# Gathers tied to TensorE's progress: two added waits before each pair of indirect DMA asks in a recommender head

## The chip, the cores and the metric

One core of one Trainium2 chip. The metric is device time in microseconds (us) from launch to end; one execution is also taken by the hardware profiler, which gives the span from the first to the last instruction. Engines: TensorE (PE; its weight loads are PEld), VectorE (DVE), ScalarE (ACT), GpSimd (POOL), SyncE (SP), and 16 DMA engines.

## What is computed

2,048 (user, item) pairs. Both indices pick an embedding row of 32 numbers; two small layers with ReLU follow, and a head over 1,250 items with a sigmoid:

```python
all_embed = jnp.concatenate([users_emb_w[users], items_emb_w[items]], axis=1)   # 2048 x 64
h = jax.nn.relu(all_embed @ w1.T + b1)                                          # 2048 x 128
h = jax.nn.relu(h @ w2.T + b2)                                                  # 2048 x 128
cross = jax.nn.one_hot(items, NUM_ITEMS, dtype=h.dtype)
head_in = jnp.concatenate([cross, h], axis=1)
return jax.nn.sigmoid(head_in @ w_head.T + b_head)                              # 2048 x 1250
```

All in float32. The one-hot part of the head is a lookup: it adds row `items` of the transposed head weights to the logits. The host lays each item's embedding and its head row side by side in `item_rows` (1,282 numbers), so one gather brings both.

## The kernel before

The 2,048 pairs are 16 tiles of 128 (`TILES`, `LAST` = 15), one pair to a partition. For tile t the work is a line through all engines:

- POOL (lines 155 to 172 of the profile's numbering) asks for two indirect DMAs: the item rows (L165, 128 rows of 5,128 bytes) and the user rows (L169, 128 rows of 128 bytes), both into tile t's own place in `rows`. Both raise the semaphore `s_rows[t]` by 16 when they have landed. Before the item ask of tile t stands one wait, on the landing of both gathers of tile t-4 (`IN_FLIGHT` = 4). POOL does nothing else after its first microseconds. `rows` has room for all 16 tiles, so no ask waits for a buffer.
- DVE `split_emb(t)`: waits for `s_rows[t]` at 32 and for `s_xT`, casts the embedding into a high part (L204, tile `emb`) and subtracts for the low part (L206). PE `transpose(t)` (L298, into `ps_x`) raises `s_xT`; DVE `copy_embT(t)` (L210) takes it to `embT`.
- PE `layer_1(t)` (L306 and L307, into `ps_h`): the second matmul raises `s_l1`. ACT `relu_1` (L259), PE `layer_2` (L311), ACT `relu_2` (L263, L268), DVE `split_h2` (L214).
- PE, the head: four passes (L315) of three matmuls each into `acc`: bias, high x high, high x low, low x high. DVE `add_rows` (L223) adds the gathered head row, ACT `sigmoid` (L273) follows, and SP writes the tile out (L150), in halves for tiles 0 to 14. Tile 15 is done in three column chunks; ACT asks for the last write (L292).

All orders are written out by hand. In PE's loop, for t from 1 to 14: bias pass of t, layer 1 of t+1, high pass of t, layer 2 of t+1, high-low pass of t, transpose of t+2, low pass of t. DVE's loop: `add_rows(t-1)`, `split_emb(t+2)`, `copy_embT(t+2)`, `split_h2(t+1)`. Semaphores `s_xT` and `s_l1` rise by one a tile, in the order of tiles.

Of the kernel before, what the change touches and what calls it, by code (L numbers as in the profile page):

```python
# [8 lines left out]
IN_FLIGHT = 4  # L9
# [10 lines left out]
def rec_head_kernel(nc, pairs, user_rows, item_rows, w1T, b1, w2T, b2, w_hiddenT, b_head, out):  # L20
# [30 lines left out]
    with ExitStack() as ctx:  # L51
# [6 lines left out]
        def sem(name):  # L58
            return ctx.enter_context(nc.semaphore(name))
# [52 lines left out]
        s_xT = sem("s_xT")  # L112
        s_embT = sem("s_embT")
        s_l1 = sem("s_l1")
# [19 lines left out]
        @block.sync  # L134
        def _(sp):
            sp.dma_start(idx[:], pairs_v).then_inc(s_idx, 16)
            sp.dma_start(bias_f[:], bias_v).then_inc(s_bhead, 16)
            for half in range(2):
                sp.dma_start(w1T_f[half * K1:(half + 1) * K1, :], w1T).then_inc(s_w1, 16)
            sp.dma_start(w2T_sb[:], w2T).then_inc(s_w2, 16)  # L140
            sp.wait_ge(s_const, 3)
            sp.wait_ge(s_bias_split, 2)
            for r, part in enumerate((bias_hi, bias_lo)):
                sp.dma_start(bias_parts[r:r + 1, :].bitcast(F32).rearrange("a (p c) -> a p c", p=BP),
                             part[:].bitcast(F32)).then_inc(s_bias_row, 16)

            for t in range(TILES):
                for i, (c, n) in enumerate(parts[t][:-1] if t == LAST else parts[t]):
                    sp.wait_ge(s_prob, parts_until(t - 1) + i + 1)
                    sp.dma_start(out_v[:, t * N + c:t * N + c + n], logits(t, c, n)).then_inc(s_out, 16)  # L150
            sp.wait_ge(s_out, 16 * parts_until(LAST))

        @block.gpsimd
        def _(pool):
            nc.gpsimd.memset(ident[:], 0.0).then_inc(s_zero, 1)
            pool.wait_ge(s_zero, 1)
            nc.gpsimd.affine_select(out=ident[:], in_=ident[:], compare_op=ALU.not_equal, fill=1.0, base=0,
                                    pattern=[[-1, P]], channel_multiplier=1).then_inc(s_ident, 1)
            pool.wait_ge(s_idx, 16)
            for t in range(TILES):  # L160

                if t >= IN_FLIGHT:
                    pool.wait_ge(s_rows[t - IN_FLIGHT], 32)
                at = t * ROW
                nc.gpsimd.indirect_dma_start(  # L165
                    out=rows[:, at + UD:at + ROW], out_offset=None, in_=item_rows,
                    in_offset=bass.IndirectOffsetOnAxis(ap=idx[:, 2 * t + 1:2 * t + 2], axis=0),
                ).then_inc(s_rows[t], 16)
                nc.gpsimd.indirect_dma_start(  # L169
                    out=rows[:, at:at + UD], out_offset=None, in_=user_rows,  # L170
                    in_offset=bass.IndirectOffsetOnAxis(ap=idx[:, 2 * t:2 * t + 1], axis=0),
                ).then_inc(s_rows[t], 16)
# [241 lines left out]
```

## Time and profile before

| | |
|---|---|
| three runs | 66.87, 66.89, 67.44 us (median 66.89) |
| the profiled execution | 66.53 us, span 64.7 us |
| PE busy | 56.9 us, 88% of the span |
| DVE busy | 42.3 us, 65% |
| ACT busy | 39.4 us, 61% |
| POOL busy | 31.2 us, 48% |
| DMA | 21.86 MB, mean 338 GB/s |
| item asks, user asks | 16 and 16, 0.95 us each on POOL |

An engine's busy time says how much it did, not whether the end waited for it. The chain of waits follows the last instruction back to what released it, step by step; the time lies there. The list of waits names who waited for whom. In a timeline each line is an instruction (or several of one kind) with its start, its duration and, in brackets, the idle time of the engine before it and what ended that. "issue" there is idle time in which the engine waited for nothing that the profile shows.

### The profile page before, as it was taken

The numbers are of one execution on the slowest core, as the hardware profiler recorded it, in microseconds if no ns is written. First come the engines' busy times: TensorE is split into PE (matmuls) and PEld (weight loads), VectorE is DVE, ScalarE is ACT, GpSimd is POOL, SyncE is SP. The second block draws the span as 40 slices with busy tenths as digits, with TensorE's granted clock in tenths as the row PEclk, the third lists the DMA queues.
The fourth block names the chain that finished last, engine by engine and source line by source line (L and its number), as shares of the span: only waits on it lengthen the run. The fifth ranks groups of instructions, "written<-read, shape, count | busy, mean of one in ns | idle before, by whom it ended". The sixth has DMA issues, their size and how long they took to land.

```text
span 64.7 us, 906 instructions
## 1 busy us (share of the span) xinstructions
PE 56.9 (88%) x284; PEld 43.3 (67%) x284; DVE 42.3 (65%) x107; ACT 39.4 (61%) x85; POOL 31.2 (48%) x38
## 2 busy tenths in 40 slices
PE   0999997899999999999999999999999999996000
PEld 1444425786688888888788877888888888774000
DVE  3810227547796969696886979696968769489000
ACT  0622921426949595776959594958678595959400
POOL 4288688778868877886887787650000000000000
PEclk9999999999999999999999999999999999999955
DMA  0589989988889999999999999999999999999980
GB/s 0 54 303 305 322 330 240 245 352 181 279 238 371 411 399 417 383 371 403 407 412 414 421 400 411 413 412 418 417 410 382 393 380 386 385 382 348 379 310 28
DMA packets 8512, 21.86 MB, mean 338 GB/s; under 512 B 1596, under 2 KB 2236, under 8 KB 8508
## 3 DMA queue, kind: packets, MB, share of 16 engines
q0 software_dynamic: 2816, 10.77, 46.5%
q1 hardware_dynamic: 5116, 10.29, 42.2%
q10 hardware_dynamic: 576, 0.76, 4.0%
q8 instruction: 2, 0.03, 0.2%
q14 instruction: 2, 0.02, 0.1%
HBM read 11.56 MB, written 10.24 MB: 337 GB/s over the span
## 4 chain that ended last, share of the span: by engine, by line
PE 67%; DMA 10%; ACT 6%; DVE 5%; issue 2%; POOL 2%; ACTq 0%
PE acc L315 52%; PE ps_h L311 8%; DMA rows<-user_rows,idx 7%; ACT rows L273 4%; DVE rows L223 4%; PE ps_x L298 4%; DMA idx<-pairs 3%; PE ps_h L307 3%; PE ps_h L306 2%; POOL rows L165 2%; DVE emb L206 1%; ACT h1T L259 1%; ACT h2T_hi L263 1%; DVE emb L204 0%; ACT h2T_f L268 0%
## 5 line engine op out<-in xcount | busy, mean ns | idle before, releaser
L223 DVE TENSOR_TENSOR rows<-acc,rows 128x625 f32<-128x625 f32 (+2 forms) x33 | 24.4, 783 | 1.2 <-PE acc L315 0.2
L273 ACT ACTIVATE rows<-rows 128x625 f32<-128x625 f32 (+2 forms) x33 | 23.1, 705 | 0.9 <-DVE rows L223 0.8
L165 POOL DMA_INDIRECT rows<-item_rows,idx x16 | 15.3, 956 | 6.0 <-issue 4.6
L169 POOL DMA_INDIRECT rows<-user_rows,idx x16 | 15.3, 954 | 4.9 <-issue 4.9
L259 ACT ACTIVATE h1T<-ps_h,b_sb 128x128 f32<-128x128 f32 x16 | 5.9, 368 | 14.5 <-PE ps_h L307 14.5
L315 PE MATMUL acc<-w_hid_lo,h2T_hi 128*128 128x512 f32 (+1 forms) x45 | 12.2, 380 | 0.0
L315 PE MATMUL acc<-w_hid_hi,h2T_lo 128*128 128x512 f32 (+1 forms) x45 | 12.1, 377 | 0.0
L315 PE MATMUL acc<-w_hid_hi,h2T_hi 128*128 128x512 f32 (+1 forms) x45 | 11.7, 369 | 0.0
L315 PE MATMUL acc<-bias_parts,bias_sel 128*128 128x512 f32 (+1 forms) x45 | 11.3, 358 | 0.0
L210 DVE CAST embT<-ps_x 128x128 fp32r<-128x128 f32 x16 | 4.7, 292 | 8.5 <-PE ps_x L298 8.5
L353 PE MATMUL ps_x<-warm_pe 128*128 128x512 f32 x12 | 8.1, 849 | 1.5 <-DVE warm_pe L176 1.5
L311 PE MATMUL ps_h<-h1T,w2T_sb 128*128 128x128 f32 x32 | 7.8, 325 | 0.6 <-ACT h1T L259 0.6
L315 PEld LDWEIGHTS acc<-bias_parts,bias_sel 128*128 128x128 f32 x45 | 7.3, 189 | 1.2
L315 PEld LDWEIGHTS acc<-w_hid_hi,h2T_lo 128*128 128x128 f32 x45 | 7.5, 193 | 0.7
L315 PEld LDWEIGHTS acc<-w_hid_lo,h2T_hi 128*128 128x128 f32 x45 | 7.4, 191 | 0.7
L315 PEld LDWEIGHTS acc<-w_hid_hi,h2T_hi 128*128 128x128 f32 x45 | 7.4, 191 | 0.6
L353 PEld LDWEIGHTS ps_x<-warm_pe 128*128 128x128 f32 x12 | 3.2, 280 | 5.5 <-issue 4.1
L311 PEld LDWEIGHTS ps_h<-h1T,w2T_sb 128*128 128x128 f32 x32 | 4.8, 188 | 2.9 <-issue 0.7
L263 ACT ACTIVATE h2T_hi<-ps_h,b_sb 128x128 fp32r<-128x128 f32 x16 | 5.9, 366 | 1.2 <-PE ps_h L311 1.2
L268 ACT ACTIVATE h2T_f<-ps_h,b_sb 128x128 f32<-128x128 f32 x16 | 5.8, 360 | 0.0
L214 DVE TENSOR_TENSOR h2T_lo<-h2T_f,h2T_hi 128x128 fp32r<-128x128 f32 x16 | 4.6, 286 | 1.1 <-ACT h2T_f L268 1.1
L298 PE MATMUL ps_x<-ident,emb 128*128 128x128 f32 x16 | 4.5, 284 | 0.3 <-DVE emb L206 0.2
(35 smaller groups left out, 39.3 us busy)
## 6 DMA issues: line engine op xcount, KB each, us to landing
probs<-rows SPq DMA_DIRECT2D x30, 312.5 KB, 7.5
w_hid_f<-w_hiddenT ACTq DMA_DIRECT2D x1, 625.0 KB, 4.4
probs<-rows SPq DMA_DIRECT2D x2, 256.0 KB, 3.2
rows<-item_rows,idx POOLq DMA_INDIRECT x16, 7.0
rows<-user_rows,idx POOLq DMA_INDIRECT x16, 7.2
probs<-rows ACTq DMA_DIRECT2D x1, 113.0 KB, 3.7
w1T_f<-w1T SPq DMA_DIRECT2D x2, 32.0 KB
w2T_sb<-w2T SPq DMA_DIRECT2D x1, 64.0 KB, 4.6
```

The source lines that it names most:

```text
L165: nc.gpsimd.indirect_dma_start(out=rows[:, at + UD:at + ROW], out_offset=None, in_=item_rows, in_offset=bass.IndirectOffsetOnAxis(ap=idx[: ...
L169: nc.gpsimd.indirect_dma_start(out=rows[:, at:at + UD], out_offset=None, in_=user_rows, in_offset=bass.IndirectOffsetOnAxis(ap=idx[:, 2 * ...
L210: nc.vector.tensor_copy(embT[:], ps_x[:, 0:P]).then_inc(s_embT, 1)
L223: nc.vector.tensor_tensor(logits(t, c, n), acc[t % SLOTS][:, c:c + n], logits(t, c, n), ALU.add).then_inc(s_sum, 1)
L259: nc.scalar.activation(h1T[:], ps_h[:, 0:P], ACT.Relu, bias=b1_sb[:]).then_inc(s_h1, 1)
L263: nc.scalar.activation(h2T_hi[t % SLOTS][:], ps_h[:, P:2 * P], ACT.Relu, bias=b2_sb[:]).then_inc(s_h2_hi, 1)
L268: nc.scalar.activation(h2T_f[:], ps_h[:, P:2 * P], ACT.Relu, bias=b2_sb[:]).then_inc(s_h2, 1)
L273: nc.scalar.activation(logits(t, c, n), logits(t, c, n), ACT.Sigmoid).then_inc(s_prob, 1)
L298: nc.tensor.transpose(ps_x[:, 0:P], emb[:], ident[:]).then_inc(s_xT, 1)
L311: nc.tensor.matmul(ps_h[:, P:2 * P], w2T_sb[:], h1T[:], start=True, stop=True).then_inc(s_l2, 1)
L315: last = nc.tensor.matmul(acc[t % SLOTS][:, c:c + n], h, w[:, c:c + n], start=first, stop=end)
L353: nc.tensor.matmul(ps_x[:], warm_pe[:, 0:P], warm_pe[:], start=True, stop=True)
```

## The change

POOL gets two more waits for each of tiles 5 to 15. Before the item ask of tile t it waits until the transpose of tile t-4 is done, beside the wait that it has on the landing of t-4; between the item ask and the user ask it waits until the first layer of tile t-4 is done. The asks themselves, their order and their destinations are the same, and no other engine's code changes.

```diff
@@ -161,11 +161,17 @@
 
                 if t >= IN_FLIGHT:
                     pool.wait_ge(s_rows[t - IN_FLIGHT], 32)
+
+
+                if t > IN_FLIGHT:
+                    pool.wait_ge(s_xT, t - IN_FLIGHT + 1)
                 at = t * ROW
                 nc.gpsimd.indirect_dma_start(
                     out=rows[:, at + UD:at + ROW], out_offset=None, in_=item_rows,
                     in_offset=bass.IndirectOffsetOnAxis(ap=idx[:, 2 * t + 1:2 * t + 2], axis=0),
                 ).then_inc(s_rows[t], 16)
+                if t > IN_FLIGHT:
+                    pool.wait_ge(s_l1, t - IN_FLIGHT + 1)
                 nc.gpsimd.indirect_dma_start(
                     out=rows[:, at:at + UD], out_offset=None, in_=user_rows,
                     in_offset=bass.IndirectOffsetOnAxis(ap=idx[:, 2 * t:2 * t + 1], axis=0),
```

## Rows read from the trace of the kernel before

**Rows 1.** The page's part 4, the chain that ended last, by engine.

```profile
PE 67%; DMA 10%; ACT 6%; DVE 5%; issue 2%; POOL 2%; ACTq 0%
```

**Rows 2.** Busy time by stretch; the last three columns are granted clock, DMA share, GB/s.

```profile
20.00:49.50 29.50, 29.50 (x171) 24.65 (x169) 23.61 (x59) 21.61 (x51) 17.42 (x19) 1.00 1.03 406
49.50:58.00 8.50, 8.50 (x47) 6.99 (x47) 6.21 (x16) 6.19 (x15) 0.00 (x0) 1.00 1.04 386
...
58.60:59.20 0.60, 0.60 (x6) 0.51 (x4) 0.60 (x2) 0.60 (x2) 0.00 (x0) 1.00 0.80 292
```

**Rows 3.** The list of waits: us in total, times, longest.

```profile
POOL rows L169 <- issue: 4.9, 16, 0.3
POOL rows L165 <- issue: 4.6, 15, 0.3
```

**Rows 4.** POOL timeline: user ask of tile 8, item ask of 10, asks of 13 to 15.

```profile
24.42 0.95 POOL L169 DMA_INDIRECT rows<-user_rows,idx  x1 [0.30 <-issue]
...
28.22 0.95 POOL L165 DMA_INDIRECT rows<-item_rows,idx  x1 [0.30 <-issue]
...
35.74 0.94 POOL L165 DMA_INDIRECT rows<-item_rows,idx  x1 [0.30 <-issue]
36.98 0.94 POOL L169 DMA_INDIRECT rows<-user_rows,idx  x1 [0.30 <-issue]
38.23 0.94 POOL L165 DMA_INDIRECT rows<-item_rows,idx  x1 [0.30 <-issue]
39.48 0.94 POOL L169 DMA_INDIRECT rows<-user_rows,idx  x1 [0.31 <-issue]
40.72 0.94 POOL L165 DMA_INDIRECT rows<-item_rows,idx  x1 [0.30 <-issue]
41.97 0.94 POOL L169 DMA_INDIRECT rows<-user_rows,idx  x1 [0.30 <-issue]
```

**Rows 5.** DVE's timeline: casts of `emb` for tiles 7, 8, 10, 11 and 15.

```profile
28.61 0.18 DVE L204 CAST emb<-rows 128x64 fp32r<-128x64 f32 x1
...
31.67 0.20 DVE L204 CAST emb<-rows 128x64 fp32r<-128x64 f32 x1
...
37.52 0.43 DVE L204 CAST emb<-rows 128x64 fp32r<-128x64 f32 x1
...
40.64 0.18 DVE L204 CAST emb<-rows 128x64 fp32r<-128x64 f32 x1
...
52.47 0.18 DVE L204 CAST emb<-rows 128x64 fp32r<-128x64 f32 x1
```

**Rows 6.** Line 169, the eight user asks from 24.3 to 42.1 us: ask to landing.

```profile
DMA to landing us min/median/max: 7.2/7.5/7.7
```

**Rows 7.** The chain in order of time, between the index's landing and POOL's first ask.

```profile
2.63 0.28 issue
```

**Rows 8.** PE's timeline: transposes of tiles 9, 10, 11, first layers of the same tiles.

```profile
35.19 0.27 PE L298 MATMUL ps_x<-ident,emb 128*128 128x128 f32 x1
...
36.52 0.27 PE L307 MATMUL ps_h<-embT,w1T_lo 128*128 128x128 f32 x1
...
38.26 0.33 PE L298 MATMUL ps_x<-ident,emb 128*128 128x128 f32 x1
...
39.64 0.28 PE L307 MATMUL ps_h<-embT,w1T_lo 128*128 128x128 f32 x1
...
41.28 0.28 PE L298 MATMUL ps_x<-ident,emb 128*128 128x128 f32 x1
...
42.61 0.27 PE L307 MATMUL ps_h<-embT,w1T_lo 128*128 128x128 f32 x1
```

**Rows 9.** Tile `emb`: all 16 casts, ns min/median/max.

```profile
L204 DVE CAST emb<-rows x16: 182/184/428, 9.1 to 52.5; 128x64 fp32r<-128x64 f32 x16
```

**Rows 10.** Landing: ACT's last write (page, part 6), and SP's 32 writes.

```profile
probs<-rows ACTq DMA_DIRECT2D x1, 113.0 KB, 3.7
...
DMA to landing us min/median/max: 2.9/7.2/12.3
```

## The prediction

> **What bounds the kernel now.** I read the page's chain of waits first, then the busy time by stretch. The chain is TensorE's own work for two thirds of the span [rows 1], and from 20 to 58 us TensorE is busy all the time [rows 2]: one matmul follows the other. What stands outside it is the start (index load, first item ask, its landing) and the end (last additions, sigmoids, last write). So the time can only move if the change makes TensorE wait, or moves the end behind the last matmul.
>
> Then the list of waits, for POOL. The idle time before its two asks is 0.3 us each time and is put down to "issue", not to a semaphore; the wait on the landing of tile t-4, which stands before each item ask, never shows as a releaser [rows 3]. POOL runs free: two asks cost 38.23 to 40.72 = 2.49 us a tile [rows 4]. The period of the other engines is read from DVE's casts of `emb`: 40.64 to 52.47 is four tiles, 2.96 us each [rows 5]. POOL gains some 0.47 us on TensorE with every tile and so is early at the end, not late.
>
> Then the DMA. From 20 to 49.5 us its share is 1.03 at 406 GB/s, and from 49.5 to 58 us, with writes alone, still 1.04 at 386 GB/s [rows 2]. It is a second limit just under the first: only at 58.6 to 59.2 us does the share dip to 0.80, when the backlog of writes is used up shortly before the last tile's come. In this load a gather of user rows lands 7.2 to 7.7 us after its ask [rows 6].
>
> **What the change adds.** Nothing is removed or moved. For tiles 5 to 15 two waits are added, 22 in all. Behind the waiting instruction on POOL stand only the later asks; SP, ACT and their queues issue nothing behind it. Who waits for the asks is DVE's cast of `emb`, then the transpose, so TensorE.
>
> *When do the waits bite?* First how fast POOL starts behind a wait: the first ask begins 0.28 us after the index landed [rows 7]. Behind a semaphore of TensorE no row shows it. I bound it by 0 below (it starts at once) and 0.30 us above, the gap before any ask [rows 4]. I take 0.28, POOL's own row.
> - Item ask 13 needs transpose 9, which ends at 35.19 + 0.27 = 35.46; plus 0.28 is 35.74. The ask of before starts at 35.74 [rows 4, 8]: delay 0. Each earlier tile has 0.47 us more of margin (tile 12 0.47, tile 5 over 3), so no earlier wait bites.
> - User ask 13 needs first layer 9: 36.52 + 0.27 + 0.28 = 37.07 against 36.98: 0.09 late.
> - Item ask 14: 38.26 + 0.33 + 0.28 = 38.87 against 38.23: 0.64 late. User ask 14: 39.64 + 0.28 + 0.28 = 40.20 against 39.48: 0.72 late.
> - Item ask 15: 41.28 + 0.28 + 0.28 = 41.84 against 40.72: 1.12 late. User ask 15: 42.61 + 0.27 + 0.28 = 43.16 against 41.97: 1.19 late. At the lower bound for the start, user ask 15 is only 42.88 - 41.97 = 0.91 us late.
>
> So the change acts on five asks of 32.
>
> *What covers the delay?* The last ask lands at 43.16 + 7.7 = 50.86 us, and the cast that reads it starts at 52.47 [rows 5, 6]: 1.6 us left. For tile 14, one tile earlier, 40.20 + 7.7 = 47.9 against 52.47 - 2.96 = 49.51: again 1.6. This would not get worse if the waits bit from tile 5 on: the ask would then follow first layer t-4 by 0.28 us, and the cast of tile t follows first layer t-1 by 40.64 - (39.64 + 0.28) = 0.72 us, three periods later: 3 x 2.96 + 0.72 - 0.28 = 9.3 us against 7.7. The landing would have to take 1.6 us longer for the cover to be gone; each us beyond is then paid once. Cost: 0.
>
> *What do the added waits cost when satisfied?* The item asks of before carry one wait, the user asks none, and the gap before both is 0.30 us (35.74 and 36.98 are such a pair) [rows 4]. The rows bound one wait to 0 to 0.01 us; above, I let a second one cost 0.05 us, a sixth of the gap, as a guess for the range. This is the place to look, since tile 8 has no reserve: asked at 24.42, landed at 31.62 at the earliest, cast at 31.67 [rows 4, 5, 6], and that cast came 0.1 us behind the pace (28.61 + 2.96 = 31.57). At 0.05 us, eight waits come before tile 8's last ask: 0.40 late. By row: 0.
>
> *DMA.* Bytes are the same. At 38 to 43 us, where the asks move by at most 1.2 us, both queues hold several us of work (gathers take over 7 us to land), so no engine of the DMA runs dry; writes get the share that gathers leave. Cost and gain 0 at the end. If some of it were gained, its bound is given under the rivals.
>
> *The phase against DVE.* One cast of `emb` is long: the one at 37.52 us took 0.43 us instead of 0.18 and ended 0.03 us after POOL's ask of 36.98 (0.94 us long) ended [rows 4, 5]. It began 0.54 us into that ask. First layers 39.64 - 36.52 = 3.12 us apart instead of 2.96 show its price on TensorE: 0.16 us [rows 8]. In the changed kernel user ask 14 starts at 40.20 and the cast follows at 40.64, 0.44 us in; for tile 15 the ask is at 43.16 and the cast at 43.60, 0.44 in again. Before, these two casts lay clear of an ask or nearly so (40.64 against 40.72). A cast that began 0.39 us into an ask (28.22 to 28.61) was not stretched [rows 4, 5], and of all 16 casts the median is 184 ns [rows 9], so overlap alone doesn't stretch one. 0.44 lies nearer to 0.39 than to 0.54. Cost between 0 and 2 x 0.16 = 0.32 us; I take 0.
>
> The Trainium skill (SBUF — State Buffer, "SBUF: two separate sides") says of the port pair that VectorE and GpSimd share that whichever starts first holds it for its whole instruction, and a copy of float32 from SBUF to SBUF is one of the instructions that need it. The stretched cast agrees with it; the unstretched ones do not, if the ask as the profile draws it is one such instruction. By the rule the sum would be 0.8 us higher, as in the third rival.
>
> **Sum.** 64.7 us span + 0 (waits) + 0 (rows in time) + 0 (DMA) + 0 (phase) = 64.7 us. The profiled execution took 66.53 us, 1.83 around its span. The median of the runs shown is 66.89, 0.36 more; with that the sum is 66.9 us.
>
> **The rivals.** About 1%, 0.67 us, is what a measurement of this kernel can tell from no change.
> - *As summed*, 66.9 us, own range 66.7 to 67.1. For it: the margins above. Chance 0.72.
> - *Casts 11 and 12 are stretched as the one at 37.52 was.* One or two times 0.16: 67.05 to 67.2 us. For it: the same order of ask and cast; against: the cast at 28.61. Within 1%. Chance 0.13.
> - *Slower: POOL's ask blocks the cast until it ends.* Cast 11 would wait from 40.64 to 41.14 and cast 12 from 43.60 to 44.10, 0.50 each. DVE absorbs part: a stretch of 0.25 cost TensorE 0.16, so 0.09 is free, and 2 x 0.41 = 0.8 us is paid: 67.7 us. It decides from 0.43 us of blocking a cast on. Against it: the cast at 28.61 lay inside an ask and took 0.18. Chance 0.04.
> - *The waits cost POOL time when satisfied.* At 0.05 us each, tile 8 lands 0.40 late and TensorE pays about that, once, since POOL gains 0.3 us a tile after it: 67.3 us. At 0.10 us each it is 0.8 and 67.7 us. Against: the equal gaps of 0.30. Chance 0.07, a third of it beyond 1%.
> - *Faster: gathers asked later leave the writes a shorter queue, and the last one lands sooner.* The last write took 3.7 us to land, the shortest of SP's writes 2.9 [rows 10]: at most 0.8 us, 66.1 us. Against: total bytes are the same and the DMA is full till 58 us [rows 2]. Chance 0.02; and 0.02 for anything else on either side.
>
> **The numbers.** Within 1%: 0.72 + 0.13 + 0.05 of the wait cost, rounded down to 0.89 for scatter. Slower: 0.04 + 0.02 + 0.01 = 0.07. Faster: 0.04. The three runs of before lie from 66.87 to 67.44, and the second rival adds 0.32, the fourth 0.4. The range goes from 66.5 (the profiled execution) to 67.4.
>
> **What would show it.** In the changed kernel's POOL timeline, asks up to tile 12 start where they did, within 0.1 us; the gap before asks of tiles 5 to 12 stays 0.30 us (a larger one is the fourth rival). The waits on TensorE appear for items 14 and 15 and users 13 to 15 alone, with the last ask near 43.2 us. DVE's cast at about 52.5 us doesn't wait for a landing. A cast of 0.4 us or more near 40.6 or 43.6 us is the second or third rival. The prediction is wrong if TensorE shows an idle time for `emb` that before does not have, if user gathers take over 9.3 us to land, or if the cast of tile 15 starts later than 52.8 us.

## The result, and the profile after

In the first comparison (20 runs each) the changed kernel takes 67.32 us, the kernel before 67.27 (medians). The ratio counts of each kernel only the runs within 1.5% of that kernel's own fastest, 17 of 20 and 12 of 20, and is 1.006 (95% interval 1.0034 to 1.0087). That is 0.4 us slower, inside the range of 66.5 to 67.4, but clear of no change, where no change was forecast. The means of all 20 runs are 67.47 and 67.37 us, 0.15% apart. In a later comparison on another chip (12 and 23 runs) the medians are 67.45 and 67.48 and the ratio is 1.0013 (0.9966 to 1.006). On two further chips the same two kernels take 72.6 or 73.0 us (changed) and 97.4 or 97.65 us (before), ratios of 0.752 and 0.749. That was in no range and in no rival, and most of what follows is about it.

The profiled execution of the changed kernel took 68.25 us, 0.9 above its median; so its extra time against the median is not the change's. Its page, with the shares by engine and the chain that ended last (part 4):

```profile
span 66.2 us, 917 instructions
...
PE 56.3 (85%) x284; PEld 43.1 (65%) x284; DVE 42.2 (64%) x107; ACT 39.3 (59%) x85; POOL 31.3 (47%) x38
...
PE 48%; DMA 23%; ACT 6%; DVE 5%; issue 5%; POOL 5%; POOLq 0%; ACTq 0%
```

The chain held 67% of PE before [rows 1]; now a gather stands in it. Its list of waits (us in total, times, longest):

```profile
POOL rows L169 <- PE ps_x L304: 5.1, 7, 1.5
POOL rows L175 <- issue: 4.3, 14, 0.3
DVE emb L210 <- DMA rows<-user_rows,idx: 3.8, 2, 2.2
...
PE ps_x L304 <- DVE emb L212: 2.2, 2, 1.4
```

The first row is the added item wait, seven times named as releaser. Five of these are delays (1.48 us once, 0.76 four times); the other two have the usual gap of 0.30 us. It answers [rows 3], where there was none. The last two rows are no work of the added waits. One of the two times in each is the first tile, at 9 us. In the other a gather of user rows, asked at 21.98 us (before: 21.92), landed late, and TensorE stood for 1.4 us. DVE's casts and PE's transposes around it:

```profile
25.77 0.18 DVE L210 CAST emb<-rows 128x64 fp32r<-128x64 f32 x1
30.37 0.20 DVE L210 CAST emb<-rows 128x64 fp32r<-128x64 f32 x1 [1.56 <-DMA rows<-user_rows,idx]
33.25 0.22 DVE L210 CAST emb<-rows 128x64 fp32r<-128x64 f32 x1
...
53.92 0.18 DVE L210 CAST emb<-rows 128x64 fp32r<-128x64 f32 x1
```

```profile
30.88 0.33 PE L304 MATMUL ps_x<-ident,emb 128*128 128x128 f32 x1 [1.36 <-DVE emb L212]
...
33.89 0.27 PE L304 MATMUL ps_x<-ident,emb 128*128 128x128 f32 x1
```

From the user ask of tile 7 to its landing (the view of line 175, for this one ask; the kernel before has 6.1 us there):

```profile
DMA to landing us min/median/max: 8.4/8.4/8.4
```

From tile 8 on, 33.25 to 53.92 is 7 tiles of 2.95 us, the pace of before [rows 5]. So the ties, once TensorE was late and they bit, cost TensorE nothing per tile. POOL's timeline shows how they bit:

```profile
20.73 0.94 POOL L169 DMA_INDIRECT rows<-item_rows,idx  x1 [0.30 <-issue]
21.98 0.94 POOL L175 DMA_INDIRECT rows<-user_rows,idx  x1 [0.31 <-issue]
...
29.57 0.94 POOL L175 DMA_INDIRECT rows<-user_rows,idx  x1 [0.30 <-issue]
32.00 0.94 POOL L169 DMA_INDIRECT rows<-item_rows,idx  x1 [1.48 <-PE ps_x L304]
33.24 0.94 POOL L175 DMA_INDIRECT rows<-user_rows,idx  x1 [0.30 <-issue]
34.95 0.94 POOL L169 DMA_INDIRECT rows<-item_rows,idx  x1 [0.76 <-PE ps_x L304]
...
45.05 0.94 POOL L175 DMA_INDIRECT rows<-user_rows,idx  x1 [0.30 <-issue]
```

Up to tile 10 the asks run back to back, as in [rows 4]. From tile 11 on each pair is one period of TensorE behind the last, and the last ask starts at 45.05 us instead of 41.97. The item ask of tile 12 starts 0.79 us behind its transpose (33.89 + 0.27 = 34.16 to 34.95), not 0.28. What the added wait does earlier, the chain in order of time shows at another transpose:

```profile
17.50 0.34 PE ps_x L304
17.85 0.02 issue
17.87 0.02 POOLq L167
```

POOLq is POOL's sequencer at the added wait. The transpose that ends at 17.83 us is tile 3's, and its wait stands before the item ask of tile 7, which the core begins at 20.73: the sequencer stood at that wait 2.9 us ahead of the core. The trace's records have the sequencer at the item wait of each of tiles 5 to 15, done 0.02 us after the semaphore rose. Its lead over the core's ask falls from 3.3 us at tile 6 to 1.6 at tile 10 and 0.75 at tile 11. So the added waits do act before tile 13, but on the sequencer's lead; they delay an ask only when the lead is used up, and then the restart costs 0.8 us. DMA share and rate by stretch (last three columns: granted clock, DMA share, GB/s) stay as in [rows 2], with TensorE's 1.4 us missing in the first:

```profile
20.00:49.50 29.50, 28.14 (x162) 23.64 (x162) 22.10 (x58) 21.05 (x49) 17.51 (x19) 1.00 1.02 396
49.50:58.00 8.50, 8.50 (x49) 7.12 (x49) 6.39 (x15) 6.20 (x16) 0.00 (x0) 1.00 1.02 385
```

### The profile page after: what moved, and what is told of

The parts are those of the page before. It is cut to its first block, busy times and chain, and to the rows that moved or that the text cites. A ratio compares the mean times of both kernels' runs of the same rounds, so it can differ in the third digit from the quotient of the medians.

```text
span 66.2 us, 917 instructions
## 1 busy us (share of the span) xinstructions
PE 56.3 (85%) x284; PEld 43.1 (65%) x284; DVE 42.2 (64%) x107; ACT 39.3 (59%) x85; POOL 31.3 (47%) x38
## 4 chain that ended last, share of the span: by engine, by line
PE 48%; DMA 23%; ACT 6%; DVE 5%; issue 5%; POOL 5%; POOLq 0%; ACTq 0%
PE acc L321 36%; DMA rows<-user_rows,idx 20%; PE ps_h L317 6%; ACT rows L279 4%; DVE rows L229 4%; POOL rows L169 3%; PE ps_x L304 3%; DMA idx<-pairs 3%; PE ps_h L313 2%; POOL rows L175 1%; PE ps_h L312 1%; DVE emb L212 1%; DVE emb L210 1%; ACT h1T L265 1%; ACT h2T_hi L269 1%
## 5 line engine op out<-in xcount | busy, mean ns | idle before, releaser
L359 PE MATMUL ps_x<-warm_pe 128*128 128x512 f32 x12 | 7.6, 800 | 1.5 <-DVE warm_pe L182 1.5
L210 DVE CAST emb<-rows 128x64 fp32r<-128x64 f32 x16 | 3.1, 195 | 3.8 <-DMA rows<-user_rows,idx 3.8
```

The source lines that it names most:

```text
L359: nc.tensor.matmul(ps_x[:], warm_pe[:, 0:P], warm_pe[:], start=True, stop=True)
```

## The experiments

Eighteen runs of fifteen kernels, on five occasions. The expectations name theories by letter, in the order in which they were formed: A, POOL is held behind TensorE whenever a gather lands late; B, each added wait costs POOL time; C, no difference beside the scatter of landings; D, gathers that fill the DMA hold TensorE's increments; E, the tie helps because it lets the gather queue run empty; F, POOL's asking holds them, whatever it brings; G, how far POOL's sequencer runs ahead of its core holds them; M, only gathers without writes beside them do. "Increment" is the rise of a semaphore at an instruction's end.

### First occasion: the change again, nothing, satisfied waits, one tie

r_after is the changed kernel, r_same the kernel before, word for word.

> The changed kernel again, for a second trace and more runs. Theory A (POOL is held behind TensorE whenever a gather of tiles 6 to 10 lands late): 1.003 to 1.009 of the kernel before, late waits bite before tile 13 only where one transpose came late. Theory B (each added wait costs POOL time even when satisfied): the gaps before the asks of tiles 5 to 10 exceed 0.30 us. Theory C (there is no difference, only the scatter of landings): 0.997 to 1.003.

> The kernel before against itself, word for word. Every theory: 1.000; what it shows beyond that is what the comparison can tell apart. Theory C expects a deviation here as large as that of the changed kernel (0.004 to 0.006).

e_satisfied:

```diff
-                    pool.wait_ge(s_xT, t - IN_FLIGHT + 1)
+                    pool.wait_ge(s_xT, 1)
...
-                    pool.wait_ge(s_l1, t - IN_FLIGHT + 1)
+                    pool.wait_ge(s_l1, 1)
```

> The same 22 waits, each on the value 1 of its semaphore, reached before 15 us, so that none can hold POOL. Theory A: 1.000 of the kernel before, no delay of asks. Theory B: 1.004 to 1.008 as in the changed kernel. Theory C: 1.000.

e_item_only, against the changed kernel:

```diff
-                if t > IN_FLIGHT:
-                    pool.wait_ge(s_l1, t - IN_FLIGHT + 1)
```

> Only the wait on the transpose of t-4 before the item ask. Theory A: as the changed kernel, 1.003 to 1.009, since in the trace of the changed kernel only the item waits bit (the user asks followed theirs after 0.30 us). Theory B: half, 1.002 to 1.004. Theory C: 1.000.

| kernel | us | ratio (95% interval) to before, 97.41 us |
|---|---|---|
| r_after | 72.61 | 0.752 (0.749 to 0.756) |
| r_same | 97.20 | 1.006 (0.998 to 1.013) |
| e_satisfied | 97.53 | 1.004 (0.994 to 1.014) |
| e_item_only | 73.50 | 0.761 (0.757 to 0.766) |

On this chip the kernel before takes 30 us more than on the first, and no theory had it. The trace of r_same, waits first:

```profile
DVE embT L210 <- remote: 29.6, 2, 21.9
...
ACT h2T_hi L263 <- remote: 14.8, 2, 10.2
...
ACT h1T L259 <- remote: 10.4, 2, 6.4
```

"remote" means that the semaphore rose at a time at which no instruction of the profile ended. DVE's copy of `embT` waits for nothing but the transpose. PE's timeline and then DVE's:

```profile
30.42 0.41 PE L298 MATMUL ps_x<-ident,emb 128*128 128x128 f32 x1
```

```profile
25.82 0.23 DVE L206 TENSOR_TENSOR emb<-rows,emb 128x64 f32<-128x64 f32 x1
47.97 0.29 DVE L210 CAST embT<-ps_x 128x128 fp32r<-128x128 f32 x1 [21.92 <-remote]
```

The transpose ended at 30.83 us, as the profile models it, and DVE started at 47.97. The trace's own record of `s_xT` has the rise at 47.94, so DVE wasn't slow: the increment came 17.1 us late. The same with `s_l1` and ACT. First PE, then ACT, then PE again:

```profile
13.32 0.28 PE L307 MATMUL ps_h<-embT,w1T_lo 128*128 128x128 f32 x1
```

```profile
16.38 0.37 ACT L259 ACTIVATE h1T<-ps_h,b_sb 128x128 f32<-128x128 f32 x1 [3.96 <-remote]
```

```profile
16.80 0.49 PE L311 MATMUL ps_h<-h1T,w2T_sb 128*128 128x128 f32 x2 [2.58 <-ACT h1T L259]
```

PE to ACT took 2.8 us (13.60 to 16.38), ACT to PE 0.05 (16.75 to 16.80). In that trace late increments are seen of TensorE alone: by 2.8 to 17.1 us between 13 and 48 us, and by 0.01 to 0.02 afterwards. Not every rise is recorded there: the trace of the kernel before holds 1,741 records of semaphores, this one 1,219, and some of DVE's and ACT's are missing too. That theirs come in time is therefore read from those who waited, as above. On the first chip the trace of the kernel before has all of TensorE's within 0.02 us. By stretch:

```profile
14.00:48.00 34.00, 7.71 (x25) 5.41 (x23) 2.47 (x7) 3.21 (x8) 21.87 (x24) 0.55 0.86 264
48.00:88.00 40.00, 39.69 (x219) 33.52 (x220) 30.61 (x78) 28.50 (x65) 0.00 (x0) 0.96 0.52 199
```

While POOL gathers, TensorE works 7.7 of 34 us; the granted clock is 0.55 there, near the lower level of 1.2 GHz. It fell at 17.4 us, after TensorE had stood idle from 14.2 to 16.8 us. The 30 us are lost here; behind it TensorE runs at its pace. In r_after it is over sooner:

```profile
16.83 0.94 POOL L175 DMA_INDIRECT rows<-user_rows,idx  x1 [0.30 <-issue]
20.67 0.94 POOL L169 DMA_INDIRECT rows<-item_rows,idx  x1 [2.90 <-remote]
21.91 0.94 POOL L175 DMA_INDIRECT rows<-user_rows,idx  x1 [0.30 <-issue]
```

```profile
12.00:21.00 9.00, 4.77 (x19) 3.46 (x19) 2.16 (x8) 1.07 (x5) 4.88 (x6) 0.75 0.82 233
21.00:62.00 41.00, 40.97 (x227) 34.15 (x227) 31.39 (x80) 29.46 (x68) 18.52 (x20) 0.97 0.98 359
```

The held increments of TensorE now hold POOL too. It pauses, and from 21 us on they come promptly again, although gathers and writes then fill the DMA (share 0.98). What is left is 4.2 us of TensorE's time between 12 and 21 us. The satisfied waits of e_satisfied do nothing of this, so where the change helps, it helps by biting; the item tie alone gives nearly all. Theory B is not settled by e_satisfied's time, whose interval (0.994 to 1.014) holds B's 1.004 to 1.008. It falls by the gaps, which are 0.30 us before all asks of that trace but the first.

### Second occasion: less in flight, slower asks, a looser tie

r_after2 is the changed kernel. The edits of d_inflight2 and d_paced, against the kernel before, and of d_tie6, against the changed one:

```diff
-IN_FLIGHT = 4
+IN_FLIGHT = 2
```

```diff
+                if t >= 2:
+                    nc.gpsimd.memset(filler[:, t * 256:(t + 1) * 256], 0.0)
                 at = t * ROW
```

```diff
+TIE = 6
...
-                if t > IN_FLIGHT:
-                    pool.wait_ge(s_xT, t - IN_FLIGHT + 1)
+                if t > TIE:
+                    pool.wait_ge(s_xT, t - TIE + 1)
```

(and `s_l1` likewise).

> The changed kernel once more, beside the kernel before on the chip of this call. Where the kernel before takes about 67 us: 1.00 to 1.01 by every theory. Where it takes about 97 us, as in the call before: 0.75 again. In either, TensorE's increments of its semaphores are the thing to read: within 0.02 us of the instruction's end, or us late.

> The kernel before with IN_FLIGHT = 2: POOL waits for the landing of tile t-2 instead of t-4 and is not tied to TensorE. Theory D (TensorE's increments are held while the DMA is full of gathers, whoever paces them): where the kernel before takes 97 us, a shorter queue of gathers helps, below 85 us. Theory E (what helps is the tie to TensorE, since it lets the gather queue run empty when TensorE is late): no tie, no help, 93 to 98 us. On a chip where the kernel before takes 67 us both expect 67 to 70 us, since a landing takes 7 us there and two tiles in flight are 7/2 = 3.5 us a tile, more than the 2.96 us of a period.

> The kernel before with one POOL memset of 128x256 before each pair of asks from tile 2 on (into a place of its own, for nothing but its time, some 0.3 to 0.6 us), no tie. Asks then come every 2.8 to 3.1 us. Theory D: where the kernel before takes 97 us, the DMA gets pauses and TensorE's increments pass, below 80 us. Theory E: 90 us or more. Where the kernel before takes 67 us: 66.5 to 70 us by both, as tiles 7 and 8 have no reserve.

> Both added waits, but six tiles back instead of four, from tile 7 on. Theory E: where the kernel before takes 97 us, between it and the changed kernel, 75 to 82 us, since the queue runs empty two tiles later. Theory D gives the same order. Where the kernel before takes 67 us: 1.000, the waits can't bite.

| kernel | us | before: 97.65 us |
|---|---|---|
| r_after2 | 72.99 | 0.749 (0.716 to 0.782) |
| d_inflight2 | 76.66 | 21 us less, no interval |
| d_paced | 93.68 | 4 us less, no interval |
| d_tie6 | 78.04 | 0.807 (0.792 to 0.823) |

Another chip, the same two speeds. d_inflight2 has no tie and still gains 21 us: E in its strict form falls. D was to get both this and d_paced, and d_paced missed it: asks 2.7 us a tile apart instead of 2.49 (POOL's timeline) still hold TensorE.

```profile
24.43 0.95 POOL L168 DMA_INDIRECT rows<-item_rows,idx  x1 [0.17 <-issue]
...
27.13 0.95 POOL L168 DMA_INDIRECT rows<-item_rows,idx  x1 [0.17 <-issue]
```

In d_inflight2 POOL's waits are those on landings, and they pause it as the ties do:

```profile
POOL rows L165 <- DMA rows<-user_rows,idx: 18.1, 10, 3.5
```

The looser tie lies between, in order: 73.0 at four tiles, 78.0 at six, 97.65 without.

### Third occasion: half the bytes, writes beside, a tighter tie, the other tie

d_half, the core of it (beside the host's narrower array):

```diff
-                    out=rows[:, at + UD:at + ROW], out_offset=None, in_=item_rows,
+                    out=rows[:, at + UD:at + K1 + HALF], out_offset=None, in_=item_rows,
...
+                    row = logits(t, c, n) if c + n <= HALF else w_hid_f[:, c:c + n]
```

d_mix:

```diff
+            sp.wait_ge(s_hidden, 16)
+            for part in scratch:
+                sp.dma_start(part, w_hid_f[:]).then_inc(s_scratch, 16)
             for t in range(TILES):
```

d_tie3 is the changed kernel with the same edit as d_tie6 and `TIE = 3`; e_user_only is the changed kernel without the wait on `s_xT`.

> The kernel before, but an item ask brings only the embedding and the first 625 head weights (2,628 bytes a row instead of 5,128); the columns from 625 on (512 on for tile 15) add another constant in place of the gathered row, so that part of the output is left wrong. POOL asks at the same pace as before. Theory D (TensorE's increments are held where gathers fill the DMA): with half the bytes the DMA has room; where the kernel before takes 97 us, below 72 us. Theory F (what holds them is POOL's asking, whatever it brings): 90 us or more. Where the kernel before takes 67 us: 66 to 67 us by both.

> Both added waits three tiles back instead of four, from tile 4 on. Where the kernel before takes 97 us: the queue runs empty earlier, at or below the changed kernel's 72 to 73 us, if the shorter lead does not cost more. Where it takes 67 us: one period of 2.96 us less lead than the 9.3 us of the changed kernel, 6.3 us against landings of 7.2 to 8.4 us, so TensorE waits in each tile until the landings shorten: 68 to 72 us.

> The kernel before with four writes of 640 KB into scratch memory, asked for by SP as soon as the head weights are there, ahead of the outputs. They bring 2.56 MB more and so at 400 GB/s 6.4 us. Theory D (a DMA full of anything holds the increments): where the kernel before takes 97 us, 97 us or more. Theory M (only gathers alone do; mixed with writes they do not, as the later stretches of all traces suggest): below 85 us. Where the kernel before takes 67 us: 71 to 75 us.

> Only the wait on the first layer of t-4 before the user ask, from tile 5 on. Theory E (either tie lets the gather queue run empty when TensorE is late): where the kernel before takes 97 us, 71 to 75 us, as with the item wait alone (73.5). Where it takes 67 us: 1.000 to 1.006.

| kernel | us | ratio to before, 97.22 us |
|---|---|---|
| d_half | 96.88 | 0.997 (0.992 to 1.002) |
| d_tie3 | 72.68 | 0.746 (0.739 to 0.753) |
| d_mix | 97.64 | 0.4 us more, no interval |
| e_user_only | 73.37 | 0.753 (0.748 to 0.758) |

The chip of the second occasion. d_half by stretch (DMA share and GB/s last):

```profile
14.00:48.00 34.00, 8.06 (x24) 6.04 (x25) 3.18 (x10) 1.97 (x5) 21.83 (x24) 0.51 0.50 134
```

The DMA is half idle and TensorE stands as long as with it full (8.06 us busy of 34, before 7.71). D falls. d_mix from 14 to 35 us:

```profile
14.00:35.00 21.00, 9.85 (x32) 7.18 (x32) 3.94 (x12) 2.77 (x8) 15.03 (x16) 0.65 1.00 363
```

Gathers and writes together at 363 GB/s, and TensorE is held all the same: M falls. Either tie alone does nearly what both do (73.5 and 73.4 us against 72.6 and 73.0). d_tie3 is no measurable gain on the changed kernel (72.68 against 72.99, at another time on the same chip). In its trace the late increments are over by 17.3 us instead of 19.9, and the granted clock is 1.00. But TensorE now stands for rows that land late (0.8 us of this is the first tile's):

```profile
PE ps_x L305 <- DVE emb L213: 2.8, 4, 1.1
```

The shorter tie leaves a landing less time, as its expectation said for a chip at 67 us.

What the traces also show, against F and G alike, is how long the hold lasts. In d_half POOL's last ask is this:

```profile
41.90 0.95 POOL L170 DMA_INDIRECT rows<-user_rows,idx  x1 [0.30 <-issue]
```

It ends at 42.85 us, and the last packet of a gather at 44.6. Yet a matmul that starts after that still raises its semaphore late. PE, then ACT, which waits for it:

```profile
45.44 0.79 PE L313 MATMUL ps_h<-h1T,w2T_sb 128*128 128x128 f32 x2 [12.27 <-issue]
```

```profile
48.56 0.37 ACT L265 ACTIVATE h2T_hi<-ps_h,b_sb 128x128 fp32r<-128x128 f32 x1 [2.56 <-remote]
```

From 46.23 to 48.56 is 2.3 us in which POOL neither asks nor has asks ahead of it. In the five traces that are held to the end (r_same, e_satisfied, d_paced, d_half, d_mix) the last late increments rise between 47.9 and 48.6 us, though the last ask ends anywhere from 42.7 to 45.5. So asking, or the lead, may start the hold; neither keeps it up at its end.

### Fourth occasion: how far POOL's sequencer is ahead

After d_half, F and G were the theories left. d_self1, against the kernel before (d_self2 has 2 for 1; v_self_tie is the changed kernel with the edit of d_self1; d_inflight3 has `IN_FLIGHT = 3`):

```diff
+                if t >= 1:
+                    pool.wait_ge(s_tick, t - 1 + 1)
                 at = t * ROW
                 nc.gpsimd.indirect_dma_start(
...
+                nc.gpsimd.memset(tick[:, t:t + 1], 0.0).then_inc(s_tick, 1)
```

> The kernel before, no tie to TensorE and no other limit on landings; but POOL writes a small tick (128x1) after each item ask, and waits for the tick of tile t-1 before the item ask of tile t. That keeps POOL's sequencer at most two asks ahead of its core and leaves the pace nearly as it was (2.6 to 2.9 us a tile). Theory G (TensorE's increments are held while many asks stand between POOL's sequencer and its core): where the kernel before takes 97 us, below 75 us. Theory F (the asks at that pace hold them, however they are handed over): 92 us or more, as with the paced kernel (93.7). Where the kernel before takes 67 us: 66.5 to 68 us.

> The same with the tick of tile t-2: at most four asks ahead. Theory G: between d_self1 and the kernel before where that takes 97 us, 75 to 95 us. Theory F: 92 us or more.

> The changed kernel with the tick of tile t-1 beside its two ties. Theory G: the asks of tiles 0 to 5, where no tie can act yet, no longer hold TensorE, so what the changed kernel still loses (5 to 6 us between 13 and 20 us) goes: 67 to 70 us where the changed kernel takes 73. Theory F: 72 to 74 us.

> The kernel before with IN_FLIGHT = 3, between 2 (76.7 us) and 4 (97 us). Theory G: a landing is awaited one tile earlier, two asks less ahead, 77 to 92 us. Theory E (only a tie to TensorE lets the queue run empty) has no place for a value between: 93 us or more.

| kernel | us | ratio to before, 67.63 us |
|---|---|---|
| d_self1 | 67.56 | 1.003 (0.998 to 1.009) |
| d_self2 | 67.06 | 1.001 (0.997 to 1.006) |
| v_self_tie | 68.16 | 0.5 us more, 4 runs, no interval |
| d_inflight3 | 67.29 | 1.002 (0.997 to 1.007) |

This chip took the kernel before in 67.6 us; nothing was held, and G against F could not be told. What it does show: limiting POOL's lead to two asks costs nothing (asks of d_self1 33.11 - 30.61 = 2.50 us a tile apart), nor does waiting for landings one tile earlier.

```profile
30.61 0.94 POOL L169 DMA_INDIRECT rows<-item_rows,idx  x1 [0.30 <-issue]
31.55 0.12 POOL L173 MEMSET tick<- 128x1 f32 x1
...
33.11 0.94 POOL L169 DMA_INDIRECT rows<-item_rows,idx  x1 [0.30 <-issue]
```

### Fifth occasion: the two open questions

r_after3 is the changed kernel, d_self1b the kernel of d_self1.

> The changed kernel again. Where the kernel before takes 67 us: theory C (no cost of its own, only the scatter of landings around tile 7) 0.997 to 1.003, with the casts of tiles 11 and later at the pace of 2.96 us; theory A 1.003 to 1.009. Where the kernel before takes 97 us: 0.75.

> The tick kernel again (POOL's sequencer at most two asks ahead of its core, no tie), which so far met only a chip where the kernel before takes 67 us (1.003). Where the kernel before takes 97 us: theory G (how far the sequencer runs ahead holds TensorE's increments) below 75 us, theory F (the asks at that pace hold them) 92 us or more.

Again a chip at 67 us: before 67.48, r_after3 67.45 (1.0013, 0.9966 to 1.006), d_self1b 67.38 (1.003, 0.999 to 1.007). Theory C's expectation holds, and A's lower end lies inside the interval too. G against F stays open. Untested is also a plain rival of both: in r_after from 21 us on asks come every 2.95 us and nothing is held, in d_paced every 2.7 us and TensorE is, and no run asks freely, without a wait that bites, at 2.95 us or slower. The casts of tiles 6 and 7 in the trace of r_after3:

```profile
26.32 0.26 DVE L210 CAST emb<-rows 128x64 fp32r<-128x64 f32 x1 [0.70 <-DMA rows<-user_rows,idx]
...
30.08 0.25 DVE L210 CAST emb<-rows 128x64 fp32r<-128x64 f32 x1 [0.72 <-DMA rows<-user_rows,idx]
```

Here two gathers landed late, before any tie could delay an ask. That much scatter is in both kernels: the runs of before spread from 66.49 to 68.42 us in the first comparison and from 66.75 to 68.5 here.

## Why the prediction was right or wrong

**The bound** was right where nothing is held: TensorE's pace of 2.95 us carries the end in both kernels.

**When the waits bite.** Two mistakes. The step took POOL's start behind a wait as 0.28 us; it measured 0.79, outside the 0 to 0.30 of the bounds. And it took the core's start as the moment of the wait, while the sequencer stands there up to 3.3 us earlier. Their joint effect on the sum is none, since the lead hides the restart until it is used up. The forecast that the core's first delay comes at tile 13 missed by two tiles (tile 11): with 0.79 in place of 0.28 the margin of 0.47 at tile 12 is already gone, and the late landing took the rest.

**The cover** was right in kind. Tied from tile 11 on, the last ask landed 7.8 us after 45.05, at 52.85, and its cast began at 53.92: 1.1 us left where 1.6 was reckoned. The difference is mostly the restart.

**The price of a satisfied wait**: 0, as taken. The gaps before the asks of tiles 5 to 10 stay 0.30 us in the changed kernel, and so they do with 22 satisfied waits. That rival falls by the gaps; the time of e_satisfied, 1.004 (0.994 to 1.014), is too coarse for it.

**The phase against DVE**: the forecast 0 holds. In lockstep casts and user asks start together (33.25 and 33.24) and a cast takes 0.22 us instead of 0.18; TensorE's period doesn't change. A whole blocking of a cast by an ask, the third rival, is not what these rows show: the ask lasts 0.94 us and the cast inside it 0.22. The Trainium skill (SBUF — State Buffer, "SBUF: two separate sides") says of this pair that whichever comes second fully blocks; if the ask is such an instruction for all its 0.94 us, these rows disagree.

**Landings** are the step that failed: the sum's term "0 (rows in time)". The text named tile 8 as without reserve and bounded a landing by 7.2 to 7.7 us, from one execution and from the asks of tiles 8 to 15 alone [rows 6]. The trace of the changed kernel has 8.4 us for tile 7, which puts TensorE 1.4 us behind, and r_after3 has two such waits, 1.1 us together on TensorE. Two of the prediction's own signs of being wrong came with it: an idle time of TensorE for `emb`, and the cast of tile 15 at 53.92, behind 52.8. The third did not (8.4 us, and 9.1 at most in r_after3, not over 9.3). It is not the ties: d_self2, which has none, shows a cast that waited 1.43 us for tile 7. The runs of the kernel before, from 66.49 to 68.42, are as wide as this. So the term was mis-sized for both kernels alike, and does not by itself make one slower than the other.

**The 0.6%.** Of the first comparison it is clear by its interval, and the second does not show it. Over all runs of the first the means differ by 0.15%, so part of the 0.6% can come from which runs are counted. The changed kernel's fastest run is 66.94 against 66.49 there and 66.92 against 66.75 here, while the medians of all runs agree within 0.05 us both times. A cost of up to 0.4 us in the runs without a late landing would fit; no trace of such a run of the changed kernel is at hand, and the cause is not shown. The traces at hand show where it is not. From the transpose of tile 8 to that of tile 15, where the ties bite, TensorE takes 20.67 us in the changed kernel and 20.65 in r_after3, against 20.92 before. From there to the end it is 11.6, 11.5 and 11.6 us. All that the two traces have more stands ahead of tile 8, where the core's asks came as before. Which term of the sum a lasting 0.6% would belong to stays open.

**What was missed altogether** is that TensorE's increments can be held while POOL gathers, on some chips. Nothing in the trace of before pointed to it, and the argument that the DMA's share makes the asks harmless could not have found it: at half the share they hold as much. Shown are: that on two chips every run of the kernel before took 95.7 to 100.4 us, and on the others 66.5 to 68.7; that in its trace there TensorE's increments come late and no other engine's are seen to; that bytes, writes beside and satisfied waits don't change it, and asks 8% slower little; and that whatever made POOL pause (a tie of three, four or six tiles, either semaphore, or landings two tiles back) shortened it, to 73 us at four tiles and 78 at six. What sets it off on one chip and not on another, and whether POOL's lead or its asking starts it, stays open; the hold outlasts both. So does what a trace can't separate: on these two chips the traces of tied kernels are short of semaphore records as well (1,169 in r_after), and whether what loses the records also delays TensorE is not tested.

## What to carry to other kernels

A wait that never bites in the trace at hand may still be what makes the kernel hold its time elsewhere: compare on more than one chip before calling it free or useless. Let an engine that only feeds others run a bounded distance ahead of them, by a tie as long as the landing asks for (here four tiles leave 53.92 - 45.05 = 8.9 us from ask to cast). Where a buffer has no reserve in one execution, take the bound of its landing from several.

## What the hardware showed unexpectedly

- TensorE's semaphore increments were up to 17.1 us late (r_same) from some 13 us on, during POOL's indirect asks and up to 5.7 us beyond the last of them (d_half: 42.85 to 48.56), on two of the chips used, while ACT's reached PE in 0.05 us.
- A wait on POOL is met by its sequencer up to 3.3 us before the core starts the instruction behind it; a core that had to wait starts 0.8 us after the semaphore's instruction ends.
- Gathers of 128 x 5,128 bytes and 128 x 128 bytes landed 3.5 to 9.1 us after the ask (traces of before and r_after3), the short ones at the start, before the first write.
